# Eight fused transformer blocks on one core: semaphores cleared inside the next stage, and no first credits for PSUM banks

## The reference

```python
x = x + _L0_xattn_ref(_layernorm(x), ctx, ctx, Wq, Wk, Wv, Wo)      # cross attention, 32 heads of 16
x = x + _L0_ffn_ref(_layernorm(x), c1_w, c2_w, w1, w2t)             # one winner in each block of 32 units
x = x + _L1_xattn_ref(_layernorm(x), ctx, Wq, Wk, Wv, Wo)           # 16 heads of 96, 4 key heads
x = x + _L1_ffn_ref(_layernorm(x), W, b, lora_A, lora_B)            # Hadamard rotation, low-rank part
x = x + _L2_xattn_ref(_layernorm(x), ctx, mask, Wq, Wk, Wv, Wo, q_norm_w, k_norm_w)  # 32 heads of 128
x = x + _L2_ffn_ref(_layernorm(x), weight)                          # rounded to 8-bit floats
x = x + _L3_xattn_ref(_layernorm(x), ctx, ctx)                      # autocorrelation by Fourier transform
x = x + _L3_ffn_ref(_layernorm(x), w1, s1, w2, s2, w3, s3)          # 4-bit weights, silu(a) * b
```

## Time and profile before

| | |
|---|---|
| time, median of 3 runs | 1523.57 us (1520.31 to 1523.79) |
| span of the profiled execution, first to last instruction | 1519.0 us (its time outside the span is not given) |
| TensorE busy | 1394.3 us, 92% |
| DVE, ScalarE, GpSimd busy | 71%, 50%, 47% |
| mean granted TensorE clock | 0.969 of full speed |

### The profile page before, as it was taken

The page is one execution under the profiler, slowest core; times in us unless marked ns, Lnnn a source line. Parts: engine busy times, 40 slices in busy tenths (PEclk is TensorE's granted clock), DMA queues, the critical chain, the costliest instruction groups (busy, mean ns, idle before and its releaser), DMA issues. The chain is left out here.

```text
span 1519.0 us, 31488 instructions
## 1 busy us (share of the span) xinstructions
PE 1394.3 (92%) x11352; PEld 830.9 (55%) x11352; DVE 1080.1 (71%) x2125; ACT 762.1 (50%) x2476; POOL 718.3 (47%) x748
## 2 busy tenths in 40 slices
PE   5798599997999999887999999999999788889998
PEld 4676244445777777444655555555555335434444
DVE  7997665645666666667989888898877779966212
ACT  4777363222434432347666666666665457655111
POOL 4888551001433434845666666665665306734000
PEclk9999799999999999999999999999999898989999
DMA  7999572215999988766775655655545401546000
GB/s 189 186 174 181 124 171 42 35 35 122 174 195 184 170 142 136 127 144 147 154 150 112 113 115 111 140 109 115 105 79 79 123 3 32 127 84 112 17 12 28
DMA packets 524570, 174.63 MB, mean 115 GB/s; under 512 B 482576, under 2 KB 507600, under 8 KB 524416
## 3 DMA queue, kind: packets, MB, share of 16 engines
q1 hardware_dynamic: 524416, 172.62, 59.0%
HBM read 53.27 MB, written 2.10 MB: 36 GB/s over the span
## 5 line engine op out<-in xcount | busy, mean ns | idle before, releaser
L1946 POOL TENSOR_TENSOR a_q_ss<-a_q_ss,half 128x4 f32<-128x4 f32 x64 | 90.1, 1408 | 167.6 <-DVE a_q_ss L1855 84.0
L67 PE MATMUL bank<-a_wq_hi,xn_pair 128*128 128x512 f16 (+1 forms) x384 | 140.8, 367 | 10.9 <-DVE a_kn L1860 5.2
L1768 ACT ACTIVATE a_probs<-a_masked,a_negmax 128x128 f32<-128x128 f32 x256 | 99.6, 390 | 101.6 <-DVE a_negmax L1826 101.6
L1285 POOL TENSOR_TENSOR a_p_hl<-a_probs,a_p_hl 128x512 f16<-128x512 f32 x64 | 74.3, 1162 | 142.3 <-DVE a_p_hl L1209 142.3
L68 PE MATMUL bank<-a_wq_lo,xn_pair 128*128 128x512 f16 (+1 forms) x384 | 140.5, 366 | 0.0
L69 PE MATMUL bank<-a_wq_hi,xn_pair 128*128 128x512 f16 (+1 forms) x384 | 140.3, 365 | 0.0
L67 PE MATMUL bank<-a_wo_hi,a_o_hi 128*128 128x512 f16 x256 | 97.8, 382 | 4.4 <-DVE x_state L1842 3.5
L68 PE MATMUL bank<-a_wo_lo,a_o_hi 128*128 128x512 f16 x256 | 97.7, 382 | 0.0
L69 PE MATMUL bank<-a_wo_hi,a_o_lo 128*128 128x512 f16 x256 | 97.5, 381 | 0.0
L1961 POOL TENSOR_TENSOR a_normal<-a_probs,a_recip 128x512 f32<-128x512 f32 x64 | 90.2, 1410 | 5.0
L716 POOL TENSOR_TENSOR a_p_hl<-a_probs,a_p_hl 128x512 f16<-128x512 f32 x64 | 78.0, 1230 | 23.6 <-DVE a_p_hl L627 16.7
(11 more groups left out here) (467 smaller groups left out, 5022.4 us busy)
## 6 DMA issues: line engine op xcount, KB each, us to landing
a_no<-in_L_xattn_Wo SPq DMA_DIRECT2D x9, 1024.0 KB, 5.7
a_nq<-in_L_xattn_Wq SPq DMA_DIRECT2D x8, 1024.0 KB, 5.8
a_n_wq<-in_L_xattn_Wq SPq DMA_DIRECT2D x4, 768.0 KB, 5.7
a_n_wo<-in_L_xattn_Wo SPq DMA_DIRECT2D x4, 768.0 KB, 6.1
a_nk<-in_L_xattn_Wk SPq DMA_DIRECT2D x9, 256.0 KB, 3.0
a_nv<-in_L_xattn_Wv SPq DMA_DIRECT2D x9, 256.0 KB, 3.1
f_v_hat<-in_L_ffn_w SPq DMA_DIRECT2D x2, 1152.0 KB, 6.2
x_state<-in_x SPq DMA_DIRECT2D x8, 256.0 KB, 5.2
```

Of the source, the lines that this page charges most:

```text
L67: pe.matmul(out, lh, rh, start=start, stop=False)
L1285: pool.tensor_tensor(p_hl[s % PN][:, 1, t, :], probs[unit(s, t) % PROBS][:, :, :].rearrange("p h n -> p (h n)"), p_hl[s % PN][:, 0, t, :], ...
L1768: m = act.activation(probs[s % 2][:, h, :], src, ACT.Exp, bias=negmax[s % 2][:, h:h + 1], accum_out=total[s % 2][:, h:h + 1])
L1946: pool.tensor_tensor(r[:, :], r[:, :], K.half[:, 0:n], ALU.pow).then_inc(root_done.sem, 1)
```

## The change

`end_stage` no longer clears or meets; it moves the stage's semaphores to a list, and `clear_before`, called on GpSimd's stream inside the next stage, clears the list. The block's own end stays. So two generations of semaphores are alive for a while. The credits are dropped everywhere: the wait for a bank's first use is left out, and the counts are one lower. The increments for the tiles made ahead go from TensorE to the head of SyncE's stream, ahead of its first two loads.

```diff
+    def wait_free(self, engine, use, turn=0):
+        n = turn * self.per[self.slot[use]] + self.nth[use]
+        if n:
+            engine.wait_ge(self.freed(use), n)
...
     def end_stage(self):
-        self.nc.clear_and_free_semaphores(self.in_use)
-        self.nc.all_engine_barrier()
-        self.in_use = []
+        self.before, self.in_use = self.before + self.in_use, []
+
+    def clear_before(self):
+        self.nc.clear_and_free_semaphores(self.before)
+        self.before = []
...
@@ every stage, TensorE @@
-                for banks in (s_bank, o_bank, q_bank, y_bank, kv_bank):
-                    for freed in banks.freed_sems:
-                        pe.sem_inc(freed, 1)
-                    pe.wait_ge(s_bank.freed(t), s_bank.n_free(t))
+                    s_bank.wait_free(pe, t)
...
@@ wide attention, SyncE, then TensorE @@
+                sp.wait_ge(first.made, len(first.MADE))
+                for use in first.MADE:
+                    sp.sem_inc(ring.filled(use), 1)
                 for kind in ("wk", "wq"):
                     load(kind, 1)
...
-                pe.wait_ge(first.made, len(first.MADE))
-                for use in first.MADE:
-                    pe.sem_inc(ring.filled(use), 1)
...
@@ GpSimd: block-wise feed-forward; second attention has t == 8, wide attention s == 12 @@
                 for t in steps:
+                    if t == CX[0] + 6:
+                        K.clear_before()
...
```

More of the change, by code:

```diff
@@ L49, in freed @@
         return self.freed_sems[self.slot[use]]
-    def n_free(self, use, turn=0):
-        return turn * self.per[self.slot[use]] + self.nth[use] + 1
+    def wait_free(self, engine, use, turn=0):
+        n = turn * self.per[self.slot[use]] + self.nth[use]
+        if n:
+            engine.wait_ge(self.freed(use), n)
     def n_filled(self, use, turn=0):
@@ L59, in n_drained @@
     def n_drained(self, use, turn=0):
-        return turn * self.per[self.slot[use]] + self.nth[use] + 2
+        return turn * self.per[self.slot[use]] + self.nth[use] + 1
 def pair_matmul(pe, out, left, right, start, stop):
@@ L88, in __init__ @@
         self.bank = [ctx.enter_context(nc.psum_tensor(f"bank{i}", [P, 512], F32)) for i in range(8)]
-        self.in_use = []
+        self.in_use, self.before = [], []
     def sem(self, name):
@@ L146, in turn @@
         ring = self.ring
-        for freed in ring.freed_sems:
-            pe.sem_inc(freed, 1)
         for b in self.uses:
             pe.wait_ge(self.xn_done.sem, self.xn_done.count(b))
-            pe.wait_ge(ring.freed(b), ring.n_free(b))
+            ring.wait_free(pe, b)
             for k in range(KT):
@@ L973, in _ @@
             def _(pe):
-                for banks in (s_bank, o_bank, ring, y_bank):
-                    for freed in banks.freed_sems:
-                        pe.sem_inc(freed, 1)
                 def tokens(t, b):
@@ L1306, in _ @@
                 for t in steps:
+                    if t == 8:
+                        K.clear_before()
                     for u in live(t):
@@ L1585, in _ @@
             def _(pe):
-                for banks in (ring, s_bank, o_bank, y_first, y_last):
-                    for freed in banks.freed_sems:
-                        pe.sem_inc(freed, 1)
                 def split_weight(kind, g):
@@ L1972, in _ @@
                 for s in steps:
+                    if s == 12:
+                        K.clear_before()
                     for use in rows_here(s):
@@ L2026, in _ @@
             def _(pe):
-                for banks in (y_bank, *up_bank, *side_bank):
-                    for freed in banks.freed_sems:
-                        pe.sem_inc(freed, 1)
                 def tile_pair(half, tiles, first, last):
@@ L2054, in tile_pair @@
                             if first and i == 0:
-                                pe.wait_ge(y_bank.freed(b), y_bank.n_free(b, half))
+                                y_bank.wait_free(pe, b, half)
                             end = last and i == len(tiles) - 1
@@ L2263, in _ @@
             def _(pe):
-                for banks in (y_bank, ring):
-                    for freed in banks.freed_sems:
-                        pe.sem_inc(freed, 1)
                 def compress(b):
@@ L2657, in _ @@
             def _(pe):
-                for freed in y_bank.freed_sems:
-                    pe.sem_inc(freed, 1)
                 for b in batches:
@@ L2873, in _ @@
             def _(pe):
-                for banks in (t_bank, y_bank):
-                    for freed in banks.freed_sems:
-                        pe.sem_inc(freed, 1)
                 pe.transpose(spread[0][0:1, 0:P], Q.big[:, 0:1], K.ident[:, :]).then_inc(in_row[0], 1)
@@ L2958, in begin @@
     def begin(self, pe):
-        for freed in self.ring.freed_sems:
-            pe.sem_inc(freed, 1)
         pe.wait_ge(self.tab, 80)
@@ L3048, in _ @@
             def _(pe):
-                for banks in (qa_bank, qb_bank, c_bank, t_bank, pr_bank, pi_bank, y_bank):
-                    for freed in banks.freed_sems:
-                        pe.sem_inc(freed, 1)
                 def queries(f):
@@ L3056, in queries @@
                     for bank, part in ((qa_bank, 0), (qb_bank, 1)):
-                        pe.wait_ge(bank.freed("x"), bank.n_free("x", f))
+                        bank.wait_free(pe, "x", f)
                         pe.matmul(bank["x"][:, :], spec[:, part, :], K.xn_rows[:, f, :],
@@ L3079, in step @@
                         for bank, part in ((pr_bank, 0), (pi_bank, 1)):
-                            pe.wait_ge(bank.freed("x"), bank.n_free("x", l))
+                            bank.wait_free(pe, "x", l)
                             pe.matmul(bank["x"][:, :], pspec[:, part, :], w_t[:, :], start=True, stop=True).then_inc(bank.filled("x"), 1)
```

65 lines of the change are left out of this document (32 added, 33 removed).

## The result

The changed kernel takes 1506.44 us (median of 4 runs, 1504.66 to 1508.87) against 1522.23 for the kernel before beside it: a ratio of 0.9909, 95% interval 0.9893 to 0.9926. A second set of runs of both gave 0.9909 again, 0.9892 to 0.9925 (experiment e5). The direction was right; the size was not.

A forecast was written before the change was run, and what follows sets the result against it. TensorE was taken to set the end wherever a stage runs long, with idle time left at seven boundaries. Gains of 0 + 0.8 + 1.7 + 2.4 + 1.6 + 1.8 + 1.5 = 9.8 us gave 1523.57 - 9.8 = 1513.8 us, range 1509 to 1519.5.

The forecast's parts named there:

- The pieces: Removed meetings and credits at the seven boundaries gain 0, 0.8, 1.7, 2.4, 1.6, 1.8 and 1.5 us, 9.8 in sum.
- The credits' price of 0.15 us each: TensorE's increments, one per PSUM bank at a stage's head, cost 0.15 us each where its next instruction waits for nothing else.
- The absorbed ones: First boundary: 1.0 us of meeting and 1.2 of credits vanish into a transfer wait; seventh: 0.5 of 2.0 us is lost.
- The forecast wait for the turned weight: Last stage: TensorE gains 1.5 us, then waits about 0.5 us for its first turned weight.
- The clears: GpSimd's drains and clears inside the next stage hide in its idle time: 0 us, bounds 0 and 1.5.
- the cover of 1.0 us: Quantised stage: GpSimd's last operation ends 1.0 us before DVE's, which hides a clear of up to two runs.
- The clock: Rival, chance 0.20: shorter third and seventh gaps keep TensorE's clock at its upper level, 2 to 3 us more, 1511 us.
- The baseline: Median time of the kernel before, 1523.57 us, 4.6 above the profiled span, from which the 9.8 us were taken.

The follow-up runs named there:

- e5: The changed kernel again with no edit: 1507.73 against 1520.99 us, ratio 0.9909.
- e2: The changed kernel with the clear and second meeting put back at each boundary, only the credits gone: 1512.65 against 1520.58 us, ratio 0.9948.
- e1: The kernel before without the second meeting, clears moved into the next stage, all credits kept: 1511.67 against 1520.58 us, ratio 0.9945.
- e3: The kernel before with idle matmuls behind TensorE's last matmul of five stages: 1520.56 against 1520.58 us, ratio 0.9995.
- e8: The changed kernel with idle matmuls at five stage tails and at four places inside stage heads: 1510.55 against 1520.99 us, ratio 0.9921.
- e7: The changed kernel with twelve increments that nobody waits for at the head of TensorE's rotated stage: 1511.83 against 1520.99 us, ratio 0.9936.
- e4: The changed kernel with idle matmuls behind TensorE's last matmul of five stages: 1507.88 us, ratio 0.9917 to the kernel before.
- e6: The changed kernel with the wait and four announcements of tiles made ahead given back to TensorE: 1508.42 against 1520.99 us, ratio 0.9911.
- e11: The changed kernel with each clear as GpSimd's first act of the next stage: 1507.32 against 1519.50 us, ratio 0.9918.
- e12: The changed kernel with a bare second meeting at every boundary, clears still inside the next stage: 1508.60 against 1519.50 us, ratio 0.9924.
- e9: The kernel before again with no edit, one run: 1520.50 us.
- e10: The kernel before once more with no edit, one run: 1520.03 us.

## Why the prediction was right and wrong

**The pieces: right.** Boundary by boundary the first work came as forecast, 9.6 us in sum for 9.8. The credits' price of 0.15 us each is borne out by e2, which keeps the meetings. The first matmul there comes 0.60 us earlier for four credits at the fifth boundary and 1.05 for seven at the sixth, and at the fourth DVE's first key tile gained 1.70 us for eleven credits and the first announcement behind them (1.6 to 1.7 forecast). The prediction chose this price against that of the Trainium skill, "TensorE: Matmul & The Clock Gate", section "The cost: per-tile semaphore tail": about 26 ns for an increment that rides on a matmul. Twelve at that price would be 0.3 us; no run here has such increments alone, and for those that ride on nothing these runs decide for 0.15.

**The absorbed ones: right at the first, wrong in kind at the last.** At the first boundary ScalarE's split came 3.50 us behind the meeting, at the transfer's landing. At the last, TensorE was to run ahead and wait 0.5 us for its first turned weight. It waits earlier, 1.45 us, for the transposed rows, whose landing in the kernel before lay at about 1336.3 + 3.3 = 1339.6 us, hidden behind credits that ended at 1340.2. The experiments agree: with the meeting back and no credits (e2), TensorE begins at the same landing, 1.41 us behind the block's own meeting, and with all credits and no second meeting (e1) the same landing releases it, at 1.68. The row of e2:

```profile
1336.30 0.38 PE L69 MATMUL bank<-xn_pair,xn_rows 128*128 128x512 f16 x1 [4.28 <-DMA xn_pair<-xn_rows]
```

The gain there was 1.1 and not 1.5. The forecast wait for the turned weight shows only where the clock stays up, in e1, e3 and e8. The step overlooked a transfer issued by the old stage's tail, the same thing that it had seen at the first boundary.

**The clears: right.** They cost nothing where they were put: in the wide attention DVE's lead over the kernel before is the same ahead of the clears and behind them. In the quantised stage GpSimd's last operation ended at 1235.39 and DVE's two behind it at about 1236.43, with the clears in between; the last clear ended at about 1236.3, so of the cover of 1.0 us some 0.1 was left:

```profile
1234.68 0.71 POOL L2790 TENSOR_TENSOR f_rstd<-f_rstd,half 128x2 f32<-128x2 f32 x1
1235.43 1.00 DVE L2860 TENSOR_SCALAR xn_rows<-x_state,f_mv,f_rstd 128x512 f32<-128x512 f32 x2 [0.52 <-POOL f_rstd L2790]
...
L109 POOLq EVENT_SEMAPHORE_RANGE_CLEAR  x2: 156/284/412, 1235.6 to 1236.2; - x2
```

They came in one to three runs each, where two to four were forecast. Against the earlier trace rows nothing moved but the start.

**The clock: the step that failed.** The sum of 9.8 us put the granted clock at nothing. The prediction had the mechanism as a rival, gave it 0.20, let it act at the third and seventh boundary, priced it at 2 to 3 us with "a little at the others", and spoke against it with the gaps of the fourth and sixth boundaries that stay near 3 us (they did: 2.73 and 2.89). It was the case that happened, and it was wider: TensorE was busy 1386 us instead of 1394 for the same work, and some 3 us of the gain go by the clock. Only at the third boundary is the whole path from the shorter gap to the clock and to the time shown by putting the gap back. The seventh gap did not shrink to 1.7 us; it grew from 3.68 to 4.32, since TensorE now ends its part of the autocorrelation 2.9 us ahead of the meeting instead of 1.2, while SyncE's last transpose is issued 1.9 us ahead of it in both.

- Third boundary: 1.69 us of TensorE, as e7 shows by putting the gap back. 1.3 had been worked out. The stage kept only 0.5 of it (2.4 us gained for 1.9 of pieces): DVE's lead over the kernel before reaches 3.55 us in the stage's middle and falls by 1.1 until its end. There the waits go through DVE, ScalarE and GpSimd, and two of GpSimd's operations take longer, a_next_rstd 0.69 us on the mean for 0.57 and a_next_shift 0.41 for 0.24 (first before, then after; the same seven instructions):

```profile
L2734 POOL TENSOR_TENSOR a_next_rstd<-a_next_rstd,half 128x1 f32<-128x1 f32 x7 | 4.0, 569 | 0.6
...
L2738 POOL TENSOR_SCALAR a_next_shift<-a_next_shift 128x1 f32<-128x1 f32 x7 | 1.7, 237 | 0.6
```

```profile
L2722 POOL TENSOR_TENSOR a_next_rstd<-a_next_rstd,half 128x1 f32<-128x1 f32 x7 | 4.8, 691 | 0.6
...
L2726 POOL TENSOR_SCALAR a_next_shift<-a_next_shift 128x1 f32<-128x1 f32 x7 | 2.8, 406 | 0.6
```

  GpSimd is slow like that, or nearly, in every profile in which neither credits nor idle increments stand ahead of the first matmul (the changed kernel, e2, e4, e5, e6, e8, e11, e12), and not in the others (before, e1, e3, e7, e9, e10). So e1, which keeps the four credits, has the shorter stage, 30.3 us for 30.7. Why the operations take longer isn't shown.

- Autocorrelation: TensorE 75.21 us before, 69.69 after. Three low-clock stretches of the kernel before: two in the stage's tail, which are gone in the changed kernel, and the one at its head, which shrank to 6.8 us. Then the changed kernel at the places of the first two:

```profile
1315.60:1322.40 6.80, 5.98 (x7) 2.52 (x8) 6.53 (x20) 4.57 (x19) 5.14 (x5) 0.50 0.87 233
...
1332.65:1336.00 3.35, 3.35 (x6) 1.27 (x5) 3.00 (x5) 0.81 (x1) 0.39 (x1) 0.50 0.81 149
1247.30:1257.45 10.15, 8.57 (x22) 5.43 (x23) 5.46 (x14) 0.60 (x1) 0.70 (x3) 0.50 0.15 10
```

```profile
1303.70:1310.50 6.80, 4.62 (x12) 1.77 (x12) 6.70 (x19) 5.31 (x21) 5.61 (x6) 1.00 0.83 232
1318.60:1322.00 3.40, 2.72 (x7) 0.93 (x5) 3.33 (x6) 0.81 (x1) 0.43 (x1) 1.00 0.80 148
```

  The stage gained 3.9 us on the mean for 1.9 of pieces. The prediction had only "a little" for it. The tail is where it shows best, by the low-clock stretch that starts 67 to 71 us into the stage. Against the first profile of before, DVE gains nothing from 71 to 86 us in e10, which has the same 6.8 us of it; 1.2 us in the four profiles with 3.4 us (e1, e6, e8 and e9, the last of them the kernel before unchanged); and 1.8 us in the eight without one (both of the changed kernel, e2, e3, e4, e7, e11, e12). So the gain goes with the clock even within one kernel, by e9 and e10. What in the change makes the stretch go isn't shown: it lies 70 us behind the boundary.
- Packed stage: 173.84 to 172.79 us of TensorE, 1.0 us; e3 shows 2.4 where the clock stays up for the whole stage. Its low-clock stretch at the head went from 6.8 to 3.4 us behind a gap that had grown, so here too the cause of the gain is the clock and the clock's own cause is open.
- Quantised stage: 0.9 us beyond the pieces on the mean, of which little can be the change. Up to its 20th microsecond DVE leads by the pieces, 1.7 us; by the 24th it gains another 0.6 and 0.3 in the two profiles of the changed kernel, loses 1.0 in e6 and 0.5 in e7, and e9, the kernel before unchanged, loses 1.2 against the first profile. The loss goes with how late the low-clock stretch at the head ends: 7.5 and 7.8 us into the stage in the changed kernel, 9.5 in e7, 10.7 in e6 and 12.4 in e9. That is a correlation.

The size for the whole kernel comes from the runs. Within each kernel, a run whose mean granted clock is higher by 0.001 is 0.63 us shorter (fit over the 105 runs of before, the changed kernel and e1 to e12 without e9 and e10, each kernel about its own mean; correlation -0.68). The kernel before had a mean of 0.9703 over 39 runs and a mean span of 1519.0 us; the changed one 0.9752 and 1505.5 over 9. That is 4.9 x 0.63 = 3.1 us by the clock, of 13.5 in all, and with the 9.6 of the pieces it makes 12.7. A mean clock lower by 0.001 is 3.0 us spent at the lower level, so a microsecond of it costs 0.2 on average. In TensorE's busy time it cost 0.5 in the rotated stage: e8, with 57 us of low-clock time in its profile for 76 and 83 in those of the changed kernel, gained nothing. That fit is a correlation, not an experiment; the experiments are e7, for one boundary, and e3, for the packed stage.

**The baseline.** This part is luck. 1523.57 us was the median of three runs; 39 more of the same kernel average 1520.7 us (a span of 1519.0). Of the 7.4 us between 1513.8 and 1506.4, 2.9 are that, and 0.8 that the changed kernel's first four runs were shorter than the mean of its nine, 1507.3. The rest, 3.7 us, is the clock and the open points below: over all these runs the gain is 13.5 us for 9.8 forecast.

**Left open.** The second attention gained about 2 us for a forecast of 0.8. Its head moves by up to 1.5 us between executions of the kernel before (the landing of wo varies there), its middle 208 us repeat to 0.02, and its tail spreads by 2.5 us over all profiles. Whether the 1.4 us beyond the meeting is an effect of the change or the luck of thirteen profiles isn't settled. Open too is 0.35 to 0.4 us in the tail of the wide stage, gained in all kernels without a second meeting and in none with one (e2 and e12 keep their shift of 1.67 and 2.06 us to the end, the changed kernel goes from 2.41 to 2.80). And it is open what, besides a gap's length, decides whether a low-clock stretch follows, on which most of the clock's part hangs.

## What to carry to other kernels

Price a removed wait by the next thing that is late, as here, and then ask a second question of TensorE: does the gap that gets shorter stand ahead of a stretch at the lower clock, and is TensorE what sets the pace in that stretch? If both, add up to half of the stretch as a case of its own with a real chance (here 1.7 us of TensorE, of which the stage kept 0.5). If TensorE isn't the pace, add nothing. Idle matmuls paid in one stage here, the packed one, and brought nothing over the whole kernel. A baseline of three runs was 2.9 us off, a fifth of the effect: take more before forecasting a change of this size. At every boundary list the transfers that the old stage's tail issued, with their landings: they, not the meeting, are next in line.

## What the runs showed of the hardware beyond that

- A bare meeting of the five engines is 0.33 us; with a GpSimd drain and clear inside it is 0.74 to 1.1.
- The low-clock stretch behind a gap is sharply repeatable in one kernel (gaps of 3.53 to 3.57 us at the third boundary in the kernel before, e9, e10 and e7, a stretch of 3.41 us each time) and not a function of the gap's length alone (2.65 us with one in e3, 2.78 without in e2; at the seventh boundary 2.59 us with one in e6, 2.86 without in e1).
- Idle matmuls raised the mean granted clock from 0.975 to 0.982 and the time by nothing or a little.
- The unchanged kernel's median over sets of 11 to 17 runs is steady to 1.5 us (1519.5 to 1521.0), but single runs spread from 1517.3 to 1525.5 us; in the profiles the spread sits in the first attention (170.5 to 174.7 us), in the head and tail of the second, in the quantised stage (42.8 to 44.1) and in which clock pattern the autocorrelation draws (90.2 or 92.1), and the wide attention's 520 us repeat to 0.05.
